# A perceiver layer on one core: early tail weights, a last head group merged head by head, and one latent product fewer

## The reference, cut to what matters

```
x = x + cross_attention(layernorm(x), ctx)      # 16 heads of 64, biases bq, bk, bv, bo; out @ Wo + bo
# second layer, 16 heads of 16, on n = layernorm(x)
q = n @ W_q ; k = n @ W_k ; v = n @ W_v
latent = (k + v) @ W_down_kv                    # 64 wide
k_rec = latent @ W_up_k ; v_rec = latent @ W_up_v
scores = q k_rec^T / 16 * exp(-0.01 |i - j|) ; attn = softmax(scores)
x = x + (attn @ v_rec) @ W_o
# third layer: gate, up and down products of fp4-rounded inputs and weights
x = x + fp4_linear(silu(gate) * up, w_down)
```

## Time and profile before

| what | value |
|---|---|
| median of 3 runs | 1438.99 us (1438.51 to 1441.53) |
| profiled execution | 1441.08 us, its span 1439.4 us |
| PE busy | 1336.4 us, 93% of the span |
| DVE busy | 1025.7 us, 71% |
| ACT busy | 882.1 us, 61% |
| POOL busy | 621.7 us, 43% |

### The profile page before, as it was taken

How to read it: one execution, slowest core, us unless ns; L and a number is a source line. 1 busy time by engine, 2 the same in 40 slices (tenths; PEclk the granted TensorE clock), 3 DMA queues, 4 the chain that set the end, 5 groups by cost and what they waited for, 6 DMA issues and landing times. The chain is left out here.

```text
span 1439.4 us, 24781 instructions
## 1 busy us (share of the span) xinstructions
PE 1336.4 (93%) x9380; PEld 1136.4 (79%) x9380; DVE 1025.7 (71%) x1407; ACT 882.1 (61%) x1716; POOL 621.7 (43%) x749
## 2 busy tenths in 40 slices
PE   5899999999999999999999999999999997489857
PEld 4788888888888888888888888888888885267734
DVE  3666678767876786678766876687668867389666
ACT  2667666666666666766666666666666664256511
POOL 5355546454645454535454555455554440000000
PEclk9999999999999999999999999999999999589979
DMA  4010000000000010100000000000000000300000
GB/s 124 16 45 2 15 1 9 8 16 1 8 9 31 2 36 30 38 30 1 9 23 1 2 8 23 1 1 8 8 1 2 1 8 1 99 0 1 1 1 15
DMA packets 25940, 22.95 MB, mean 16 GB/s; under 512 B 5472, under 2 KB 25568, under 8 KB 25824
## 3 DMA queue, kind: packets, MB, share of 16 engines
q1 hardware_dynamic: 25824, 21.39, 5.0%
HBM read 20.86 MB, written 0.52 MB: 15 GB/s over the span
## 5 line engine op out<-in xcount | busy, mean ns | idle before, releaser
L544 ACT ACTIVATE pT_hi<-psT 128x512 fp32r<-128x512 f32 x512 | 293.1, 600 | 219.6 <-PE psT L313 199.2
L619 DVE TENSOR_TENSOR pT_lo<-psT,pT_hi 128x512 fp32r<-128x512 f32 x512 | 332.5, 685 | 81.6 <-ACT pT_hi L544 75.8
L613 DVE TENSOR_REDUCE negm<-psS 128x1 f32<-128x1024 f32 x256 | 311.7, 1218 | 52.3 <-PE psS L303 52.3
L264 POOL TENSOR_TENSOR kT<-kraw,khi 64x512 fp32r<-64x512 f32 x252 | 325.0, 1290 | 0.0
L258 POOL CAST khi<-kraw 128x512 fp32r<-128x512 f32 x126 | 76.9, 610 | 510.3 <-ACT kraw L520 509.5
L510 ACT ACTIVATE prob<-psS,negm 128x1024 f32<-128x1024 f32 x256 | 285.5, 1115 | 1.0 <-DVE negm L613 1.0
L313 PE MATMUL psT<-ident,prob 128*128 128x128 f32 x2048 | 268.5, 274 | 3.9 <-DVE pT_lo L619 3.9
L329 PE MATMUL psO<-pT_hi,v 128*128 128x256 f32 x1024 | 267.5, 294 | 1.2 <-DVE pT_lo L619 0.4
L313 PEld LDWEIGHTS psT<-ident,prob 128*128 128x128 f32 x2048 | 234.3, 141 | 34.0 <-issue 7.1
L330 PE MATMUL psO<-pT_lo,v 128*128 128x256 f32 x1024 | 255.7, 282 | 0.0
L303 PE MATMUL psS<-kT,q_hi 64*128 64x512 f32 x1024 | 194.6, 416 | 3.4 <-ACT prob L510 2.0
(11 more groups left out here) (213 smaller groups left out, 1590.6 us busy)
## 6 DMA issues: line engine op xcount, KB each, us to landing
cst<-in_ctx_dram SPq DMA_DIRECT2D x12, 512.0 KB, 3.9
oT<-in_ctx_dram SPq DMA_DIRECT2D x4, 512.0 KB, 5.0
wraw<-in_L_xattn_Wk_dram SPq DMA_DIRECT2D x8, 256.0 KB, 2.6
wraw<-in_L_xattn_Wv_dram SPq DMA_DIRECT2D x8, 256.0 KB, 3.4
wraw<-in_L_xattn_Wq_dram SPq DMA_DIRECT2D x8, 256.0 KB, 2.6
wo<-in_L_xattn_Wo_dram SPq DMA_DIRECT2D x8, 256.0 KB, 2.7
ff_wdn<-in_L_ffn_w_down_dram SPq DMA_DIRECT2D x1, 704.0 KB, 8.7
ff_win<-in_L_ffn_w_gate_dram SPq DMA_DIRECT2D x1, 640.0 KB, 6.0
```

Of the source, the lines that this page charges most:

```text
L264: pool.tensor_tensor(kT[half, m // 2 % KRING, h, 1, :], raw[own, :], khi[own, :].bitcast(F32), ALU.subtract).then_inc(k_split, 1)
L544: act.activation(pT_hi[:, i % PRING, :], psT[:, t % 2, :], ACT.Copy).then_inc(ph_ok, 1)
L613: dve.tensor_reduce(negm[:, g % 2, h, qt, c:c + 1], psS[:, qt, :], AX.X, ALU.max, negate=True)\
L619: dve.tensor_tensor(pT_lo[:, i % PRING, :], psT[:, t % 2, :], pT_hi[:, i % PRING, :].bitcast(F32), ALU.subtract).then_inc(pl_ok, 1)
```

## The change

- `Tail` lays the weights, masks and tables of the second and third layer into the room of `ctxT_hi` and `ctxT_lo`. Their transfers, and POOL's masks, start once all projections are done, four steps before the end of cross attention. ACT makes the decay table between the last steps.
- `bo` is loaded into the free staging tile early on, and POOL adds it to `y` during step 12.
- The merge of the last group goes head by head: `head_max` and `head_end` for one head per step, two `post` and two `weigh_out` in each of steps 13, 14 and 15. Their sums are made by POOL, as three halvings (256, 128, 64 columns wide). Only the two merges of head 3 stay behind step 127.
- W_k + W_v is added by POOL, turned, and multiplied with W_down_kv while the last two merges run: the second block makes latent = n (W_k + W_v) W_down_kv with one product of 2 x 512 columns, and kv is gone.

```diff
@@ SP, end of the first block
+            wait(sp, k_ps, N)
+            wait(sp, v_ps, N)
+            for i, a in ((0, W_k), (1, W_v)):
+                sp.dma_start(tail.w[:, i, :, :], a.rearrange("(t p) n -> p t n", p=P)).then_inc(tail.w_in[i], 16)
...
@@ POOL
+                if n == FIRST + KT * FIRST:
+                    wait(pool, bo_in, 16)
+                    wait(pool, xn_ok, B * QT)
+                    pool.tensor_tensor(y[:, :, :], y[:, :, :], cst[:, 0, :].unsqueeze(1).to_broadcast([P, B * QT, D]),
+                                       ALU.add).then_inc(bo_ok, 1)
+            def add_out(g, k):
...
+                wait(pool, comb, 16 * g + 2 * k + 1)
+                pool.tensor_tensor(oweighed[:, 0:2, :], oweighed[:, 0:2, :], oweighed[:, 2:4, :], ALU.add)\
+                    .then_inc(part, 1)
...
+            for k in range(6):
+                add_out(GP - 1, k)
+                if k == 1:
...
+                    pool.tensor_tensor(tail.w[:, 0, :, :], tail.w[:, 0, :, :], tail.w[:, 1, :, :], ALU.add)\
+                        .then_inc(tail.kv_ok, 1)
@@ PE, in step n
+                elif k >= 13:
+                    wait(pe, comb, 16 * g + 2 * (2 * (k - 13) - 1) + 1 if k > 13 else 0)
+                    post(g, 2 * (k - 13), psW[:, :])
                 turn(n, 0)
                 turn(n, 1)
...
+                if g == GP - 1 and k >= 13:
+                    wait(pe, comb, 16 * g + 2 * 2 * (k - 13) + 1)
+                    post(g, 2 * (k - 13) + 1, psW[:, :])
                 turn(n, 2)
@@ PE, behind the last step
-            for k in range(8):
...
+            pe.wait_ge(comb, 16 * (GP - 1) + 2 * 5 + 1)
+            post(GP - 1, 6, psW[:, :])
+            pe.wait_ge(exp_ok, 2 * N)
+            post(GP - 1, 7, bank_S[0])
+            pe.wait_ge(tail.kv_ok, 1)
...
+                    last = pe.transpose(bank_T[0][:, half * D + kt * P:half * D + (kt + 1) * P],
+                                        tail.w[:, 0, kt, half * P:(half + 1) * P], ident[:, :])
...
+                    last = mm(bank_T[1][:, kt * HD:(kt + 1) * HD], tail.wkvT[:, half, kt * P:(kt + 1) * P],
+                              tail.wd[:, half, :], start=(half == 0), stop=(half == KT - 1))
@@ ACT, in and behind the last steps
+                if n == N - 3:
+                    wait(act, tail.const, 2)
+                    act.activation(tail.relf[:, :, :], tail.rel[:, :, :], ACT.Abs).then_inc(tail.decay_ok, 1)
...
@@ second block, PE
-            for d in range(KT):
-                step(("kv", d), product([(w[:, i, kt, cols(d)], xnT[:, kt, :]) for i in range(2) for kt in range(KT)]))
+            pe.wait_ge(wc_ok, 1)
+            step(("lat", 0), product([(wc[:, kt, :], xnT[:, kt, :]) for kt in range(KT)]))
@@ second block, DVE
-            dve.wait_ge(bo_in, 16)
             for r in range(R):
-                dve.tensor_tensor(y[:, r, :], y[:, r, :], bot[:, :], ALU.add).then_inc(x1_ok, 1)
```

More of the change, by code:

```diff
@@ L12, with __init__, take, cross_attention @@
 P = 128
-def cross_attention(nc, x, ctx, Wq, bq, Wk, bk, Wv, bv, Wo, ident, y):
+class Tail:
+    def __init__(self, st, nc, ctxT_hi, ctxT_lo, D, DL, F, S):
+        KT, QT, FT = D // P, S // P, (F + P - 1) // P
+        room = 2 * ctxT_hi.shape[1] * ctxT_hi.shape[2]
+        def take(name, shape):
+            nonlocal room
+            size = 1
+            for n in shape:
+                size *= n
+            room -= (size + 7) // 8 * 8
+            return st.enter_context(nc.sbuf_tensor(name, [P] + shape, F32))
+        self.w = take("sa_w", [4, KT, D])
+        self.wd = take("sa_wd", [KT, DL])
+        self.wu = take("sa_wu", [2, D])
+        self.win = take("ff_win", [2, FT, D])
+        self.wdn = take("ff_wdn", [KT, F])
+        self.wkvT = take("sa_wkvT", [KT, D])
+        self.wc = take("sa_wc", [KT, DL])
+        self.rel, self.relf, self.decay = (take(name, [QT, S]) for name in ("sa_rel", "sa_relf", "sa_decay"))
+        self.hm = take("sa_hm", [8])
+        take("ctx_rest", [room])
+        sem = lambda name: st.enter_context(nc.semaphore(name))
+        self.w_in = [sem(f"sa_w{i}") for i in range(7)]
+        self.wg_in, self.wu_in, self.wd_in, self.zero_ok = sem("ff_wg"), sem("ff_wu"), sem("ff_wd"), sem("ff_zero")
+        self.const, self.masks = sem("sa_const"), sem("sa_masks")
+        self.decay_ok, self.kv_ok = sem("sa_decay_ok"), sem("sa_kv_ok")
+        self.kvT_ps, self.kvT_ok, self.wc_ps, self.wc_ok = (sem(n) for n in ("sa_kvT_ps", "sa_kvT_ok", "sa_wc_ps",
+                                                                              "sa_wc_ok"))
+def cross_attention(nc, x, ctx, Wq, bq, Wk, bk, Wv, bv, Wo, bo, ident, y, ctxT_hi, ctxT_lo, tail, W_q, W_k, W_v, W_o,
+                    W_down_kv, W_up_k, W_up_v, w_gate, w_up, w_down):
     B, S, D = x.shape
@@ L184, in load_piece @@
                     wait(sp, prep_ps, u)
+                if b == 1 and piece == 0:
+                    wait(sp, bo_ok, 1)
                 sp.dma_start(cst[:, :, :], ctx_t[b, piece]).then_inc(cst_in, 16)
@@ L735, in _ @@
                     add_out(g - 1, k)
+                if k >= 13 and g == last_group:
+                    weigh_out(g, 2 * (k - 13) + 1, psW[:, :])
                 p_low(n, 2)
@@ L739, in _, with self_attention_and_ffn @@
                     v_low(n + LEAD, psW[:, :])
-                if k == STEPS - 2:
+                if k == STEPS - 2 and g < last_group:
                     weigh_max(g)
-                if k == STEPS - 1:
+                if k == STEPS - 1 and g < last_group:
                     weigh_end(g)
+                if k >= STEPS - GH and g == last_group:
+                    head_end(k - 12)
+                if k >= STEPS - GH - 1 and k < STEPS - 1 and g == last_group:
+                    head_max(k - 11)
                 if prep_unit(n) is not None:
                     prep_low(prep_unit(n), psW[:, :])
-            for k in range(8):
-                weigh_out(GP - 1, k, (psW[:, :], bank_S[0], bank_S[1], bank_S[2])[k % 4])
+            for k in range(6, 8):
+                weigh_out(GP - 1, k, psW[:, :] if k == 6 else bank_S[0])
                 add_out(GP - 1, k)
             add_y(GP - 1)
-def self_attention_and_ffn(nc, W_q, W_k, W_v, W_o, W_down_kv, W_up_k, W_up_v, bo, w_gate, w_up, w_down, ident, y,
-                           out):
-    D = W_q.shape[0]
+def self_attention_and_ffn(nc, tail, W_down_kv, w_gate, ident, y, out):
+    D = W_down_kv.shape[0]
     KT = D // P
@@ L975, in _ @@
                 step(("q", d), product([(w[:, 2, kt, cols(d)], xnT[:, kt, :]) for kt in range(KT)]))
-            pe.wait_ge(w_in[4], 16)
-            pe.wait_ge(proj_ok, at[("kv", 1)] + 1)
-            step(("lat", 0), product([(wd[:, kt, :], kvT[:, kt, :]) for kt in range(KT)]))
             pe.wait_ge(w_in[5], 16)
@@ L1137, in _ @@
                 copy_out(("x", kt), xnT[:, kt, :])
[L1138 to L1139 removed]
+            copy_out(("lat", 0), latT[:, :], rows=DL)
             for d in range(KT):
                 copy_out(("q", d), qT[:, d, :])
[L1142 removed]
             for d in range(KT):
```

189 lines of the change are left out of this document (111 added, 78 removed).

## The result

The changed kernel takes **1423.41 us** (median of four, 1418.52 to 1424.65); the kernel before, on the same chip, 1440.26 (1438.51 to 1445.92). The ratio is 0.987 [0.9833, 0.9907]: faster by 17 us, where the prediction said 22.2. The median lies 6.6 above the forecast and 1.9 above the range. Of the 6.6, 1.3 is the start: the forecast was counted from a median of 1438.99. The profiled execution took 1422.61 us, its span is 1421.1. The four executions spread over 6 us, and go with the mean granted clock: 1418.52 at 0.977, 1422.61 at 0.974, 1424.21 at 0.971, 1424.65 at 0.972. (In the page of before, the slice with the clock at 5 tenths and the transfers at 3 is the 35th, where PE is at 4 tenths, not the 34th.)

The account below looks back on a forecast made before the run. PE bounds the 128 steps; the change acts on the chain of waits from the last step to the second layer's first scaled score. 7.6 + 0.5 + 5.7 + 8.4 = 22.2 us less gives 1416.8 us, range 1413.5 to 1420.

Parts of the forecast that it names:

- What it gains, the whole gains.: Second layer's head loop: time gained at the first scaled score reaches the end whole, since every engine's later order is unchanged.
- rivals for the clock up to the first scores: Output products to first scores: 2.4 GHz kept, 1413.0 us, chance 0.09; or 1.2 GHz from merged steps, 1445.0, 0.02.
- The merge, 7.6 + 0.5: Behind step 127: two merges left instead of eight, 7.6 us; `turn_o` at full clock rate, 0.5 us.
- the terms of the prediction: Steps 125 to 127: DVE's added `post` and `weigh_out` lengthen 125 and 126 by 1.0 us each, 127 by 0.5.
- The lock of DVE and POOL, 0.3: Merged steps: small DVE instructions stretched by POOL's work on the shared SBUF port, 0.3 us lost, between 0 and 2.7.
- The bias, 5.7: Start of the second block: the transfer of `bo` and its four adds leave the chain, 5.7 us.
- the weights' early transfer: The tail's weights, transferred four steps earlier on an otherwise empty queue: this alone gains nothing.
- Rival 3: Second block's start: another start cost replaces the bias transfer, only adds of 1.43 us go; 1421.1 us, chance 0.04.
- The products, 8.4: Second block, first product to first scaled score: latent from one product lets DVE mask earlier, 8.4 us.
- POOL as the slow link: Merged steps: each odd `weigh_out` waits for POOL's three sums, 5.7 us lost, 1422.5 us; chance 0.11.
- The kind clock: Output products to second block: 2.4 GHz through `project_o` and up when products start, 3.8 us more, 1413.0; chance 0.09.
- A loss of clock ahead of step 127: Merged steps: extra waits thin out PE, which is granted 1.2 GHz from there on; 1445.0 us, slower; chance 0.02.

Follow-up runs that it names:

- c2: Changed kernel with three added 512-column products, result unread, ahead of the values of unit 0 in the head loop: 1417.08 us, ratio 0.9827.
- c10: Changed kernel with one added 512-column product, result unread, ahead of the values of unit 0 in the head loop: 1417.53 us, ratio 0.9831.
- c6: c2 with one more unread product ahead of the last `turn_o` and five while PE waits for the first normalised rows: 1412.78 us, ratio 0.9803.
- c11: Changed kernel with bias and latent products as before, leaving the head-by-head merge and the early transfers: 1430.56 us, ratio 0.992.
- c4: Changed kernel with the latent products as before (kv from two weights, no joined weight): 1427.82 us, ratio 0.9914.
- c7: Kernel before with only three added 512-column products, result unread, in its head loop: 1439.48 us, ratio 0.9984.
- c8: Changed kernel with the six merged weighed sums of steps 125 to 127 on DVE instead of POOL: 1426.72 us, ratio 0.9905.
- c9: Changed kernel with five added unread products only ahead of the first normalised rows of the second block: 1422.79 us, ratio 0.9867.
- c3: Changed kernel with the last group's eight merges again behind step 127, sums on DVE: 1432.23 us, ratio 0.9937.
- c5: Changed kernel with the bias transferred and added in the second block, as before: 1430.29 us, ratio 0.9917.

## Why the prediction was wrong, point by point

- **"What it gains, the whole gains."** This step failed. The order of the instructions behind the first scaled score is the same in both kernels, but the clock is not: 5.5 us were given back, 4.1 in units 4 to 6, where the clock was at 0.50 for 13.7 us and not 3.4, and 1.4 behind the last unit. c2, c10 and c6 take the 4.1 away by adding work. The 1.4 stay in c2 (85.51), are 0.2 in c10 (84.08) and gone in c6 (83.72). I had rivals for the clock up to the first scores and none behind them. The rest of the miss is the start of 1438.99, 1.3 under the 1440.26 measured with the result.
- **The merge, 7.6 + 0.5.** Right in size. The last sum ends 7.5 earlier after the shift of the steps ahead is taken off, and the output products give 0.6 more; c11 has 7.9 for both. In the steps it is partly luck: from the third turn of one step to that of the next (124 to 127) the distances grew by 0.7, 0.7 and 1.5 us, where the terms of the prediction give 0.5, 1.0 and 1.0: 3.0 in all, where 2.5 and 0.3 for the lock were put. In step 127 `post` waits 0.56 for ACT's `oT`, since no scores lie between (the row at 1207.42).
- **The lock of DVE and POOL, 0.3.** It happens, and cost nothing in the end. A `wts` of DVE took 1.22 us beside POOL's sum of W_k and W_v, and 0.17 without it (shown above), as the Trainium skill has it (SBUF — State Buffer, section SBUF: two separate sides); this one event made the first maximum of step 126 late by 0.3. The second came 16.53 us behind the second of step 124, and so it did in c4, which has no sum of W_k and W_v: the step had made it up.
- **The bias, 5.7.** Right in sum (5.7 from the add to the statistics), wrong in kind: 1.35 of it (1.5 in c11) comes with the weights' early transfer, of which I had said that it gains nothing. Rival 3 (the block waits for something else) did not come: the statistics begin 0.33 behind the add.
- **The products, 8.4.** Near in size (7.9 in the trace, 8.3 by c4), but 2.7 of it is clock, and so luck: the traces of before and c4 have a second stretch at 0.50 between the first product and the first score, and c7 and c11, with the same products, do not (19.69 and 19.58 us in place of 22.33). Against these the one product is worth 5.2 to 5.3.
- **The rivals.** POOL as the slow link did not come: its sums take 0.73, 0.47 and 0.32 us, and c8 shows them worth 4.3 at the merge's end. The kind clock did not come by itself; c6, which forces it, gains from add to first score 3.2 us (1224.18 to 1243.04 against 1224.77 to 1246.87), and 1.65 in the output projection. A loss of clock ahead of step 127 did not come (it is 1.00 until 1220).

What stays open: why the clock stays at 0.50 for 3.4 us in one kernel and 10, 14 or 17 in another, behind the same idle stretch of 2.7 us and with PE busy all the while. The two kernels with 3.4 (before, c4) had another stretch at 0.50 that ended about 7 us earlier; the others had none so near. That is a coincidence of two traces, not a cause. With the clock as it falls, the parts of the change do not add up: against before, the merge alone gives 10 to 11 us, with the products 11, with the bias 13, and all three 17 to 20. The Trainium skill (TensorE: Matmul & The Clock Gate, Part 1: The HAM clock gate) says that from run to run one kernel has different numbers of products at the lower clock after its start. The traces of before and c7 show the like at a later place: between the first product and the first scaled score the same instructions had 8.7 us at 0.50 in one and 3.1 in the other. The two levels of the changed kernel's times would fit that; no run here has a trace of its faster executions.

## What to carry to other kernels

Carry a saving to the end of the program only after asking of each later stretch whether PE's idle time in it goes with a fall of the granted clock; a change in front can make that fall last longer without changing an instruction. Where PE waits some microseconds and then has a chain bound by it, one product that nobody reads can give back more than it costs (3 to 6 us here for 0.9 us of work), but not if it is still running when the waited-for data comes (c9: no gain in time), and less where the clock falls for a short time only (c7: 2 us for three products). And before a stretch of a trace is priced, read its granted clock in more than one execution: some 2.7 of the 22.2 us here were the clock of one execution, and the match of two medians hid it.

## What was not expected of the hardware

- After a fall, the clock stayed at 1.2 GHz for 13.5 to 17 us while PE was busy for 13.50 of 13.50 and 17.00 of 17.00 us (c9, c3), with short products of 16, 128 and 256 columns.
- In c10 the clock stayed at 1.00 over 20.00 us in which PE was busy 14.59; what went with the falls in the other kernels was the one wait of 2.7 us, of which c10 fills a third.
- A broadcast transfer of 1 KB rows for the bias took 3.0 us on quiet queues and made DVE wait 3.33 (c5), and 4.4 and 4.68 when the weights were issued right behind it (before).
- The same instructions of one kernel, from the first product to the first scaled score, took 22.33 and 19.69 us in two traces (before, c7), with 8.7 us at 1.2 GHz in the first and 3.1 in the second.
